# Perceiver layer on one Trainium2 core: tile loops written out, cross attention's lists reordered, its maximum taken in pieces

## What is computed

```python
kvx = jnp.einsum('bsi,oi->bso', cond, w_kv_x)          # cond: 1601 context rows per batch
kx, vx = jnp.split(kvx, 2, axis=-1)
kx = _ln(kx.reshape(b, sc, g, d), kxln_w, kxln_b)      # 8 groups of 128
scores = jnp.einsum('bsghd,btgd->bghst', q, k) * scale
p = jax.nn.softmax(scores, axis=-1)                    # over 1601
xout = jnp.einsum('bghst,btgd->bsghd', p, v)
```

## Time and profile before

| | |
|---|---|
| median of 3 runs | 2833.57 us (2833.2 to 2834.51) |
| profiled execution, its own time | 2834.08 us |
| its span | 2832.3 us |
| TensorE matmul busy | 2291.5 us (81%) |
| VectorE busy | 2108.2 us (74%) |
| ScalarE busy | 1552.4 us (55%) |
| GpSimd busy | 1568.4 us (55%) |
| first start of TensorE's scores in cross attention | 533.4 us |
| mean granted TensorE clock | 0.919 |

### The profile page before, as it was taken

How to read it: one execution, slowest core, us unless ns; L and a number is a source line. 1 busy time by engine, 2 the same in 40 slices (tenths; PEclk the granted TensorE clock), 3 DMA queues, 4 the chain that set the end, 5 groups by cost and what they waited for, 6 DMA issues and landing times. The chain is left out here.

```text
span 2832.3 us, 55857 instructions
## 1 busy us (share of the span) xinstructions
PE 2291.5 (81%) x18514; PEld 1816.5 (64%) x18514; DVE 2108.2 (74%) x4502; ACT 1552.4 (55%) x3129; POOL 1568.4 (55%) x1619
## 2 busy tenths in 40 slices
PE   2466652799999999999999999999999999856556
PEld 1243341578778777777777777777777788644334
DVE  8888984577787877878786787778778777658763
ACT  4455451566666666666666666666666666411211
POOL 2465565667676667667666666666666664340000
PEclk7677776999999999999999999999999999977778
DMA  2000103100101111110101011010111100073100
GB/s 104 16 38 30 44 23 121 59 26 31 44 32 32 38 32 34 42 33 32 38 32 32 34 42 33 32 44 26 32 34 42 32 9 2 1 256 105 35 18 8
DMA packets 74545, 120.03 MB, mean 42 GB/s; under 512 B 21168, under 2 KB 56576, under 8 KB 73216
## 3 DMA queue, kind: packets, MB, share of 16 engines
q1 hardware_dynamic: 74240, 116.23, 12.3%
HBM read 94.20 MB, written 22.02 MB: 41 GB/s over the span
## 5 line engine op out<-in xcount | busy, mean ns | idle before, releaser
L71 PE MATMUL x_kc<-x_wk,x_ctxT 128*128 128x256 f16 x4992 | 626.8, 275 | 71.2 <-POOL x_ctxT L975 40.6
L997 POOL TENSOR_TENSOR x_kT<-x_kf,x_kT 128x512 f16<-128x512 f32 (+1 forms) x448 | 629.3, 1405 | 37.4
L995 POOL TENSOR_SCALAR x_kT<-x_kf 128x512 f16<-128x512 f32 (+1 forms) x448 | 285.8, 638 | 619.2 <-ACT x_kf L1067 617.1
L71 PE MATMUL x_ox<-x_ctxp,x_pt 128*128 128x256 f16 x4992 | 619.5, 273 | 0.0
L71 PEld LDWEIGHTS x_kc<-x_wk,x_ctxT 128*128 128x128 f16 x4992 | 484.5, 98 | 155.5 <-issue 59.6
L71 PEld LDWEIGHTS x_ox<-x_ctxp,x_pt 128*128 128x128 f16 x4992 | 486.1, 98 | 72.1 <-issue 11.3
L1055 ACT ACTIVATE x_kraw<-x_kc 128x512 f32<-128x512 f32 (+1 forms) x448 | 254.0, 567 | 429.1 <-PE x_kc L71 217.3
L1263 DVE TENSOR_REDUCE x_ss<-x_sq 128x4 f32<-128x512 f32 (+1 forms) x448 | 283.0, 642 | 232.4 <-ACT x_sq L1059 230.8
L1320 DVE TENSOR_TENSOR x_pt<-x_tp,x_pt 128x512 f16<-128x512 f32 (+1 forms) x512 | 297.9, 585 | 116.9 <-ACT x_pt L1094 113.4
L1067 ACT ACTIVATE x_kf<-x_tp,x_hv 128x512 f32<-128x512 f32 (+1 forms) x448 | 330.1, 754 | 86.1 <-PE x_tp L1146 85.3
L1181 PE MATMUL x_tp<-x_ident,x_pb 128*128 128x128 f32 x1664 | 256.5, 274 | 56.5 <-ACT x_pb L1088 54.3
(11 more groups left out here) (234 smaller groups left out, 3180.4 us busy)
## 6 DMA issues: line engine op xcount, KB each, us to landing
x_stage<-in_ctxT SPq DMA_DIRECT2D x32, 800.5 KB, 4.4
x_stage<-in_ctx SPq DMA_DIRECT2D x16, 896.0 KB, 5.1
x_stage<-in_ctx SPq DMA_DIRECT2D x16, 640.0 KB
scr_q<-a_qxT SPq DMA_DIRECT2D x8, 1024.0 KB, 3.9
x_qs<-scr_q SPq DMA_DIRECT2D x16, 512.0 KB, 5.3
scr_core<-a_catc SPq DMA_DIRECT2D x8, 512.0 KB, 2.6
scr_x<-x_catx SPq DMA_DIRECT2D x8, 512.0 KB, 2.7
f_area<-in_wprojT SPq DMA_DIRECT2D x4, 1024.0 KB, 11.0
```

The lines of the kernel that those rows point to most:

```text
L71: last = pe.matmul(out, lhs[i], rhs[j], start=start and n == 0, stop=stop and n == len(parts) - 1)
L995: gp.tensor_scalar(dst[0], src, 1.0, 0.0, ALU.mult, ALU.add).then_inc(khi_ready, 1)
L997: gp.tensor_tensor(dst[1], src, dst[0], ALU.subtract).then_inc(kT_ready, 1)
```

## The change

All ten hardware loops over tiles (five engines, two stages) become Python loops, so the tiles are written out and semaphore values are constants. In cross attention TensorE does ("pv", -1, 2) before ("pt", 0, 0) instead of after; VectorE does ("pt", 1, 1) before the root chain instead of after its third instruction, and ("quant", 3) after ("m", 4) and ("oa", -1); in steps of jj = 1 to 3 GpSimd does pieces 0 to 2 before unit 0 and piece 3 before unit 2; in steps of jj = 0 the place of the pieces stays. VectorE's maximum is taken in three reductions (65, 1024 and 512 elements) with a small maximum between, and a new semaphore tells when the first two banks of scores are there.

```diff
@@ the ten loops over tiles of the first two stages, all like this one @@
-            with sp.Fori(0, TILES - 1) as t:
+            for t in range(0, TILES - 1):
...
@@ -738,8 +738,8 @@
-        m1 = sb("m1", [P, 2])
-        m2 = sb("m2", [P, 2])
+        m3 = sb("m3", [P, 2, 3])
+        mall = sb("mall", [P, 2])
...
+        sc_two = sem("sc_two")
...
@@ ORDER (TensorE) @@
-                 ("tr", 1), ("ob", -2), ("pt", 0, 0), ("pv", -1, 2), ("pt", 0, 1), ("m", 2), ("tr", 2), ("pt", 0, 2),
+                 ("tr", 1), ("ob", -2), ("pv", -1, 2), ("pt", 0, 0), ("pt", 0, 1), ("m", 2), ("tr", 2), ("pt", 0, 2),
...
@@ DVE_ORDER @@
-                     ("quant", 2), ("m", 3), ("max", 1), ("quant", 3), ("m", 4), ("oa", -1), ("m", 5), ("quant", 4),
-                     ("ob", -1), ("pt", 1, 0), ("m", 6), ("rs", 0), ("rs", 1), ("rs", 2), ("pt", 1, 1), ("rs", 3),
+                     ("quant", 2), ("m", 3), ("max", 1), ("m", 4), ("oa", -1), ("quant", 3), ("m", 5), ("quant", 4),
+                     ("ob", -1), ("pt", 1, 0), ("m", 6), ("pt", 1, 1), ("rs", 0), ("rs", 1), ("rs", 2), ("rs", 3),
...
@@ GpSimd @@
+            def convert_one(t, j, n):
+                jj, b = j % SPB, t * BT + j // SPB
+                rows, half = jj < 2, jj % 2
+                slot = (j // SPB + 1) % 2 if rows else (j // SPB) % 2
+                if n == 0 and rows and not (first(t) and j < 2):
+                    gp.wait_ge(pv_done, b * 8)
+                if n == 0 and not rows:
+                    gp.wait_ge(kc_filled, (b + 1) * SPB * KU)
+                per_b = 3 if half else 2
+                loads = (4 if half else 3) + b * per_b + ((2 if half else 1) if rows else per_b)
+                convert_piece(rows, half, b, slot, loads, n, 24 + b * 16 + jj * 4 + n + 1)
...
+                    early = [0, 0, 0, 2] if jj else [2, 3, 4, 5]
                     for i in range(KU):
+                        for n in [n for n in range(4) if early[n] == i and jj and convert_here]:
+                            convert_one(t, j, n)
                         if exists(t, j, ("tr", i)):
                             split_unit(JK, j + 1, i)
-                        if i >= 2 and i < 6 and convert_here:
-                            n = i - 2
...
+                        for n in [n for n in range(4) if early[n] == i and not jj and convert_here]:
+                            convert_one(t, j, n)
...
@@ TensorE, the scores @@
+                        if n == 1:
+                            ins.then_inc(sc_two, 1)
                     ins.then_inc(sc_done if kind == "sc" else sr_filled, 1)
...
@@ VectorE, the maximum @@
                 elif kind == "max":
                     A_ = o[1]
+                    v.wait_ge(sr_ready, J * 2 + A_ + 1)
+                    v.tensor_reduce(m3[:, A_, 2:3], srem[:, A_], X, ALU.max).then_inc(m_chain, 1)
+                    v.wait_ge(sc_two, J * 2 + A_ + 1)
+                    v.tensor_reduce(m3[:, A_, 0:1], s3[:, 0:1024], X, ALU.max).then_inc(m_chain, 1)
+                    v.wait_ge(m_chain, (J * 2 + A_) * 4 + 2)
+                    v.tensor_tensor(mall[:, A_:A_ + 1], m3[:, A_, 0:1], m3[:, A_, 2:3], ALU.max).then_inc(m_chain, 1)
                     v.wait_ge(sc_done, J * 2 + A_ + 1)
-                    v.tensor_reduce(m1[:, A_:A_ + 1], s3[:], X, ALU.max).then_inc(m_chain, 1)
-                    v.wait_ge(sr_ready, J * 2 + A_ + 1)
-                    v.tensor_reduce(m2[:, A_:A_ + 1], srem[:, A_], X, ALU.max).then_inc(m_chain, 1)
-                    v.wait_ge(m_chain, (J * 2 + A_ + 1) * 2)
-                    v.tensor_scalar(negm[:, A_:A_ + 1], m1[:, A_:A_ + 1], m2[:, A_:A_ + 1], -SOFTMAX_SCALE, ALU.max,
+                    v.tensor_reduce(m3[:, A_, 1:2], s3[:, 1024:1536], X, ALU.max).then_inc(m_chain, 1)
+                    v.wait_ge(m_chain, (J * 2 + A_ + 1) * 4)
+                    v.tensor_scalar(negm[:, A_:A_ + 1], mall[:, A_:A_ + 1], m3[:, A_, 1:2], -SOFTMAX_SCALE, ALU.max,
                                     ALU.mult).then_inc(negm_ready, 1)
```

More of the change, by code:

```diff
@@ L352, in _ @@
             keep_core(0)
-            with gp.Fori(1, TILES - 1) as t:
+            for t in range(1, TILES - 1):
                 split_heads(t + 1)
@@ L464, in _ @@
             tile(0, True, True)
-            with act.Fori(1, TILES - 2) as t:
+            for t in range(1, TILES - 2):
                 tile(t, True, True)
@@ L544, in _ @@
             tile(0, True, True)
-            with pe.Fori(1, TILES - 2) as t:
+            for t in range(1, TILES - 2):
                 tile(t, True, True)
@@ L681, in _ @@
             tile(0, True)
-            with v.Fori(1, TILES - 2) as t:
+            for t in range(1, TILES - 2):
                 tile(t, True)
@@ L945, in _ @@
             tile(0)
-            with sp.Fori(1, TILES - 1) as t:
+            for t in range(1, TILES - 1):
                 tile(t)
@@ L1111, in _ @@
             tile(0)
-            with act.Fori(1, TILES - 1) as t:
+            for t in range(1, TILES - 1):
                 tile(t)
@@ L1226, in _ @@
             tile(0)
-            with pe.Fori(1, TILES - 1) as t:
+            for t in range(1, TILES - 1):
                 tile(t)
@@ L1380, in _ @@
             tile(0)
-            with v.Fori(1, TILES - 1) as t:
+            for t in range(1, TILES - 1):
                 tile(t)
```

## The result

The change makes the kernel slower: 2848.60 us (median of 5 runs, 2846.23 to 2852.09) against 2834.51 us (5 runs of the kernel before on the same chip, 2833.20 to 2838.44), a ratio of 1.0048, 95% interval 1.0036 to 1.0059. The forecast was 2825 us, faster. The time lies within 2785 to 2860, the range given with it, but slower than the kernel before instead of faster.

What follows compares the result with a forecast made beforehand. The chain from M, the end of the last sum of squares, to "pt" 0,1 was taken to set the cross-attention step. From 2834.1 us, -24 - 7 + 28 - 6 = -9 gave 2825 us, range 2785 to 2860.

Steps and rivals of the forecast that it cites:

- Back edges and register instructions: Cross attention: five taken branches removed, -24 us; constant values instead of registers in 48 looped steps, -7 us.
- third rival: All written-out tiles: late instruction fetches in longer straight code keep the branches' cost; 2849 us, chance 0.08.
- Self-attention: First stage's loops: straight code saves nothing there, 0, with ±9 us for the clock of six tiles.
- GpSimd holds the root chain: VectorE's root chain under early pieces: "norm" 0 at M + 5.8 (features) or 6.0 (rows); transitions together +28 us.
- first rival: Early pieces in cross attention cost nothing; all transitions at 11.5, -45 for +28; 2752 us, chance 0.13.
- three pieces now follow the last unit at once: GpSimd, three of four steps: last unit over at M + 0.42, pieces then end at M + 5.0 and M + 5.2.
- The maximum, +0.32 on the chain: VectorE's maximum in cross attention: reductions in a row take 2.45 us against 2.13; early start unused.
- the chain's 7.33: Cross attention, from "norm" 0 to "pt" 0,1: maximum, exponentials and ScalarE's copy take 7.33 us.
- "pt" 1,1 first, 0: VectorE before the root chain: scores start some 0.6 us earlier, root chain 0.7 later but hidden; together 0.
- "pv" -1,2 first: TensorE before "pt" 0,0: fills 0.85 us, but "pt" 0,1 still waits for ScalarE's copy; gives only -0.2.
- "Quant" 3, -6 us: VectorE, moved behind "m" 4 and "oa": removes TensorE's wait for "oa", 15 × 0.4, between -5 and -8 us.
- second rival: Root chain into jj = 1, 2, 3: one VectorE operation per GpSimd operation, "norm" 0 at M + 6.9; 2871 us, chance 0.16.

Runs made afterwards that it cites:

- the straight code: Only the ten tile loops written out as Python loops, against the kernel before the change; 2801.52 us, ratio 0.9876.

## Why the prediction was wrong

- *Back edges and register instructions, -31 us.* Right in sum: -33.3 in the kernel that does only that, though the constants give some 13 of it and not 7. With no "issue" wait left the third rival (the branches' cost stays) is out.
- *Self-attention, 0.* Right: the first scores of cross attention start at 533.8 us, before at 533.4.
- *GpSimd holds the root chain, one operation slips in per piece.* Right: into jj = 3 the forecast was M + 5.8 and M + 13.1, measured 5.85 and 13.13. By the Trainium skill (SBUF — State Buffer, SBUF: two separate sides) the port pair that VectorE and GpSimd share is an exclusive lock: of a VectorE instruction with two SBUF inputs and a GpSimd one that reads SBUF, the one that starts first has it for the whole instruction. The operations under the pieces agree, with 0.81 us for one that takes 0.19 alone. The first rival (the pieces cost nothing) is out.
- **The step that failed: "in three of four steps three pieces now follow the last unit at once", with the last unit's end at M + 0.42 for all of them.** I took that from a step of the last tile, which has neither pieces nor a "quant". It holds only into jj = 3. Into jj = 1 the last unit is over at M + 1.59, because the pieces of jj = 0 stay between units; the trace of before showed that (the low part of the last unit from 1046.17 for 0.70 us, against M = 1045.30), and I hadn't looked there. Into jj = 2 it is M + 1.27, because "quant" 4 holds unit 5. "Norm" 0 came at M + 6.70 and 6.67, past the M + 6.3 that the prediction had named as a sign of being wrong, and "pt" 0,1 at 13.98 instead of 13.4 and at 13.96 instead of 13.1: 15 × 0.58 + 14 × 0.86 = 21 us. Of the 0.86, about 0.45 is not the unit but "pt" 1,1 (below).
- *TensorE's clock.* In steps of jj = 2 TensorE starts its scores early ("pt" 1,1 first) and then waits 2.1 us for "on", which stands behind the seventh operation of the held root chain. In three of these steps it came back at half its clock: 3 × 1.29, 4 us that no term held.
- *The maximum, +0.32 on the chain.* Measured +0.26, and 11 us for the kernel; in the forecast's sum it was inside the chain's 7.33, which measured 7.28.
- *"pt" 1,1 first, 0.* Wrong: with the pieces where they now are it costs 9 us, all of it part of the two points above.
- *"pv" -1,2 first, -0.2 a step.* The gap between ScalarE's copy and "pt" 0,1 agrees, 0.05 us instead of 0.28. No run has this part alone, so it is not shown.
- *"Quant" 3, -6 us.* The gain came, 0.41 us a step against the straight code. With the pieces at their old places the move does bring it (17.74 us for 18.09), as forecast; but the early pieces bring it without the move, so in the changed kernel the move itself adds nothing.

2825 + 21 + 4 = 2850, less the 2 us by which the loops gave more: 2848, against 2848.24 of the profiled execution. That it meets to the microsecond is luck. From "pt" 0,1 to M the steps take 17.68 us against 17.62 in the straight code, 62 × 0.06 = 4 us that are in no term and that I can't explain, and the stretch behind the last M was shorter than before (407.1 us, 409.5 before). The second rival (one operation by one, 2871 us) named the right place: the transitions with pieces are 0.49 us over the forecast on average, past the 0.21 at which the change is worth nothing. Its mechanism did not occur: into jj = 3 an operation slips in between a high and a low part, as forecast.

## What to carry to other kernels

Where the operations of two engines hold each other up, every small operation becomes part of the schedule: what counts is not how much work GpSimd has but which of VectorE's operations are dependent and small while it runs, and when its own queue gets there. Take the start of a moved block from each place where it will stand, not from one of them. And weigh a wait by what it does to the chain that sets the step: here 63 us of waits could be removed with a loss of 18, while moving four pieces of work that nobody waited for gave 90 us (2837.6 to 2747.7).

## What I had not expected of the hardware

- The hold goes both ways, by who comes first: VectorE's 1.22 us operation stretched a GpSimd one from 0.62 to 1.47 us, as a GpSimd piece stretched VectorE's from 1.22 to 2.08. A VectorE operation that reads PSUM (the maximum, 1.75 us) ran at full speed beside a piece.
- TensorE's clock. In two steps of jj = 2 of the changed kernel TensorE had been idle for the same 2.10 us:

```profile
966.67 4.32 PE L71 MATMUL x_ox<-x_ctxp,x_pt 128*128 128x256 f16 x24 [2.10 <-DVE x_on L1340]
...
1091.30 2.79 PE L71 MATMUL x_ox<-x_ctxp,x_pt 128*128 128x256 f16 x24 [2.10 <-DVE x_on L1340]
```

The windows over these products (us, busy times by engine, granted clock next to the DMA share) show full clock, 2.4 GHz, in the second (1.00) and, for much of the first (0.62), 1.2 GHz:

```profile
966.67:971.00 4.33, 4.33 (x26) 3.39 (x26) 4.16 (x11) 1.09 (x2) 0.15 (x1) 0.62 0.00 0
1091.30:1094.00 2.70, 2.70 (x25) 2.44 (x26) 2.60 (x8) 0.42 (x1) 0.15 (x1) 1.00 0.00 0
```

What decides between the two after the same idle time stays open: 3 of 13 such steps fell in the changed kernel, 5 of 13 in the one with the maximum of before, 9 of 13 in the one whose row pieces of jj = 0 came sooner.
- Straight code several times as long showed no cost: the kernel with only the loops written out came within 2 us of its forecast, with no "issue" wait on TensorE in cross attention.
